# TensorE's first branch-prefetch hint stands two token pairs earlier, and the code ahead of it is aligned anew

## The reference

```python
logits = tokens @ gate_weight.T
top1 = argmax(logits); mask = one_hot(top1)
ranks = cumsum(mask, axis=0) - 1          # place of a token within its expert
mask = mask * (ranks < 320)
dispatch = gather of each expert's tokens
out = scatter( gelu(dispatch @ wi[e]) @ wo[e] * softmax weight )
```

## Time and profile before

| | |
|---|---|
| median of 3 runs | 1103.7 us (1102.2 to 1104.22) |
| the profiled execution | 1102.2 us |
| its span | 1100.5 us |
| mean granted TensorE clock | 0.978 |
| TensorE busy | 1044.6 us (95%) |
| instruction fetches on queue q8 | 31 packets, 0.51 MB |

### The profile page before, as it was taken

One profiled execution on the slowest core, in us unless ns is written; L12 is line 12 of the kernel. 1 busy time (PEld: TensorE's weight loads), 2 busy tenths in 40 slices (PEclk: granted clock), 3 DMA queues, 4 the chain that ended last, 5 costly groups with the idle time before them and its releaser, 6 DMA issues.

```text
span 1100.5 us, 20923 instructions
## 1 busy us (share of the span) xinstructions
PE 1044.6 (95%) x7912; PEld 989.0 (90%) x7912; DVE 721.5 (66%) x1089; ACT 543.9 (49%) x851; POOL 147.4 (13%) x135
## 2 busy tenths in 40 slices
PE   7699999999999999599999996999999999999995
PEld 5699999999999999378777766999999999999995
DVE  7556565776577686478685765557767677665652
ACT  5345455565556565263332224455656656554431
POOL 2201111203021110100000022002112031130101
PEclk9799999999999999899999998999999999999998
DMA  8468546565464750500011235436566565654410
GB/s 308 175 229 309 183 168 211 193 219 205 159 233 158 256 200 38 177 1 1 1 39 39 77 106 186 145 123 243 181 229 228 191 243 179 226 211 144 170 38 24
DMA packets 83280, 177.38 MB, mean 161 GB/s; under 512 B 4192, under 2 KB 4704, under 8 KB 83168
## 3 DMA queue, kind: packets, MB, share of 16 engines
q1 hardware_dynamic: 75488, 152.61, 39.1%
q0 software_dynamic: 7168, 23.07, 5.8%
q10 hardware_dynamic: 576, 1.05, 0.3%
HBM read 162.04 MB, written 18.87 MB: 164 GB/s over the span
## 4 chain that ended last, share of the span: by engine, by line
PE 92%; DVE 2%; DMA 2%; ACT 1%; issue 1%; POOL 1%; POOLq 0%; SPq 0%; ACTq 0%; DVEq 0%
PE psH L1213 13%; PE psH L1214 13%; PE psH L1215 13%; PE acc L1220 12%; PE acc L1221 12%; PE acc L1222 12%; PE acc L1213 3%; PE acc L1215 3%; PE acc L1214 3%; PE psT L1433 1%; PE psT L1269 1%; PE acc L1389 1%; PE psH L1389 1%; PE psT L1538 1%; PE psH L1440 1%
## 5 line engine op out<-in xcount | busy, mean ns | idle before, releaser
L1213 PE MATMUL psH<-dth,wih 128*128 128x240 f32 (+5 forms) x1024 | 294.6, 288 | 0.0
L1220 PE MATMUL acc<-hth,woh 128*128 128x240 f32 (+5 forms) x1024 | 293.4, 287 | 0.0
L1221 PE MATMUL acc<-htl,woh 128*128 128x240 f32 (+5 forms) x1024 | 293.2, 286 | 0.0
L1222 PE MATMUL acc<-hth,wol 128*128 128x240 f32 (+5 forms) x1024 | 293.2, 286 | 0.0
L1215 PE MATMUL psH<-dth,wil 128*128 128x240 f32 (+5 forms) x1024 | 293.2, 286 | 0.0
L1214 PE MATMUL psH<-dtl,wih 128*128 128x240 f32 (+5 forms) x1024 | 293.1, 286 | 0.0
L787 DVE TENSOR_TENSOR wol<-raw_wo,woh 128x1024 fp32r<-128x1024 f32 x128 | 155.7, 1223 | 146.6 <-ACT woh L609 146.6
L643 ACT ACTIVATE gel<-psH 128x320 f32<-128x320 f32 x256 | 111.9, 437 | 188.9 <-PE psH L1215 183.7
L609 ACT ACTIVATE woh<-raw_wo 128x1024 fp32r<-128x1024 f32 x128 | 134.3, 1056 | 132.3 <-PE acc L1222 132.2
L1213 PEld LDWEIGHTS psH<-dth,wih 128*128 128x128 f32 x1024 | 192.8, 188 | 0.3
L1220 PEld LDWEIGHTS acc<-hth,woh 128*128 128x128 f32 x1024 | 192.8, 188 | 0.0
(11 more groups left out here) (194 smaller groups left out, 1151.3 us busy)
## 6 DMA issues: line engine op xcount, KB each, us to landing
raw_wi<-in_wi SPq DMA_DIRECT2D x64, 1024.0 KB, 5.1
raw_wo<-in_wo SPq DMA_DIRECT2D x64, 1024.0 KB, 5.4
out_x<-xt SPq DMA_DIRECT2D x4, 1024.0 KB, 5.8
xt<-in_x SPq DMA_DIRECT2D x6, 512.0 KB, 8.0
xt<-x SPq DMA_DIRECT2D x3, 1024.0 KB, 10.5
raw_u<-in_wuT SPq DMA_DIRECT2D x1, 1024.0 KB, 10.8
raw_u<-in_wvT SPq DMA_DIRECT2D x1, 1024.0 KB, 12.5
xt<-in_x ACTq DMA_DIRECT2D x2, 256.0 KB, 3.4
```

Source lines behind the costliest of these rows:

```text
L1213: pe.matmul(out, lh, rh, start=first, stop=False)
L1220: pe.matmul(out, lh, rh, start=False, stop=False, skip_group_check=True)
L1221: pe.matmul(out, lh, rl, start=False, stop=False, skip_group_check=True)
L1222: return pe.matmul(out, ll, rh, start=False, stop=False, skip_group_check=True)
```

## The change

Hint 1 is marked at `p == 4` instead of `p == 6`, and the alignment constant goes from 35 to 153:

```diff
-TO_HINT = 35
+TO_HINT = 153
...
                         if p >= 2:
                             folds(p - 2)
-                        if p == PAIRED - 2:
+                        if p == 4:
                             peek()
```

## The result

The kernel after takes 1110.25 us (median of 5 runs, 1107.79 to 1110.61), the kernel before 1103.45 us (5 runs beside them, 1102.11 to 1104.22). The ratio is 1.0059, with a 95% interval of 1.0045 to 1.0075: 6.8 us more, where I had forecast 2.4 us less. The profiled execution of the kernel after took 1108.56 us, with a span of 1106.8 us and a mean granted clock of 0.975.

The account below looks back on a forecast made before the run. TensorE bounds the kernel; only its stall ahead of the first expert can shrink. Short branch 1 gives -2.4 us, alignment and thinner visit cover cost nothing: 1103.7 to 1101.3 us, range 1100.1 to 1105.6, the forecast's own 1100.1 to 1103.1.

Parts of the forecast that it names:

- The hint is served in time: Ahead of branch 1: hint at about 12.6, packet between 19.1 and 22.0, so the branch is short; chance 0.50.
- The range I took: Wait of the visit's fetch behind its hint while DMA engines are full: 6.5 to 9.4 us.
- The step that failed: At the boundary 17 instructions behind branch 1: block C, asked for at 10.3, is there in time; cost nothing.
- rival C: Behind branch 1: hint replaces block C's request, a stall of 2.7 us beside a late branch, 1106.4 us; chance 0.12.
- rival D: Ahead of L1389: remaining visits bind, 1.5 us for two visits, 0.9 us of gain left, 1102.8 us; chance 0.04.
- a cap: At L863: of the 4.13 us stall only 2.4 us can be had, the rest becomes a wait for VectorE.
- if the clock falls all the same: Table products ahead of the first expert: even if the granted clock drops to half, the gain stays 2.4 us.
- Rival A: At branch 1: hints bring nothing, the branch asks for its block itself and waits as before, 1103.7 us; chance 0.18.

Follow-up runs that it names:

- e3: Kernel before with hint 1 at p = 4 and alignment constant 205, so the hint is 7 instructions past a block boundary; 1110.54 us, ratio 1.0066.
- e12: Kernel after with the third and fourth visits of the first FFN exchanged; 1121.68 us, ratio 1.0179.
- e9: Kernel after without the fourth visit of the first FFN; 1108.42 us, ratio 1.0048.
- e6: Kernel before with branch 1 moved behind take_counts(), hint 1 and alignment kept; 1103.07 us, ratio 1.0009.
- e10: Kernel before without the fourth visit of the first FFN; 1101.21 us, ratio 0.9986.

## Why the prediction was wrong

- **The hint is served in time: right, and sooner than I put it.** The hint was expected at 12.6 and stands at 12.5; branch 1 takes 0.33 us. But its packet starts at 16.31, 3.8 us after it, not after 6.5 to 9.4 us. It is 3.8 us again in e3 (16.81 to 20.56) and in e12, and 3.7 us in e9, with a DMA share of 1.04 to 1.05 each time, as before. The range I took, 6.5 to 9.4 us, was too late; two more kernels with the hint where it was before, e6 and e10, have 5.6.
- **The step that failed** is the sentence "block C must be in the store when the boundary behind branch 1 is passed ... It is asked for at 10.3 and has 12 us. This costs nothing." It wasn't fetched at all until the return from the visit. I had the sign of it in the earlier trace rows, where block L wasn't fetched while hint 1 was pending, and weighed it as rival C with 0.12, since the hint is 2.2 us younger than the boundary. The runs show that 2.2 us isn't enough for the block's own request to get ahead, and that it is ahead when the hint stands 80 instructions in or more.
- **Rival C happened, and was priced too low.** Its 2.7 us were to stand beside a branch as long as before. From the return's end (22.84) it took 1.8 us to the first packet (24.67), 2.5 us until both packets, side by side, were done (27.20), and 1.7 us to the eighth product (28.92): 6.1 us, of which the seven products cover 0.6, so 5.46 us of stop. Branch 1 is short as well, so `earlier()` starts 3.56 us sooner (23.09 for 26.65), and 1.9 us are left at L1308.
- **What lies behind L1308.** The table products take 6.27 us for 5.80 us, 0.5 us more; the clock, at half from 28.6 to 32 before, stays there until 34.9. The stretch 32 to 35.4 after, columns as in the earlier trace rows:

```profile
32.00:35.40 3.40, 3.40 (x20) 3.40 (x20) 2.83 (x3) 0.00 (x0) 0.67 (x1) 0.58 0.03 5
```

  The last normalized rows are ready 2.6 us later than before, and then the visits bind, as rival D had it: the sequencer's L1479, at 40.6 in the earlier trace rows, is behind them now, at 44.9, since branches 3 and 4 took 4.4 and 3.4 us. That is the last 0.5 us of 3.12.

```profile
L1479 PEldq FUSED_REGOPS  x1: 53/53/53, 44.9 to 44.9; - x1
```

- **Nothing in the prediction held the 4.1 us at the third expert.** I let the effect on the store end with the first expert. 2.56 us of it is the miss, the rest the clock at half for 3.4 us after the stop.
- **The gain had a cap that I had seen, and it was too high.** I put 2.4 us on a short branch 1. The kernel with the visit behind the counts has no stop at all, and its ratio is 1.0009. The 2.4 us are there at L863, but I let everything behind it move along by the same amount, also "if the clock falls all the same". In fact the table products wait 0.7 us for VectorE and take 0.5 us more at the low clock, and 1.1 us arrive at L1389. In 13 of the 14 kernels a packet starts between 22.4 and 25.5 us, hint or not, which is about where the DMA share falls from 1.0; that it is what bounds this stage was only argued, not tried.
- **Rival A's half truth.** Where it stood, hint 1 made branch 1 no shorter, though leaving it out costs 0.2% (1.0022 [1.0011, 1.0033]). But hints aren't dead: in the kernel with the visit behind the counts the hint turns 3.7 us into 0.33.

The Trainium skill's page "Runtime: NRT & Kernel Launch", section "Instruction fetch mechanics", has prefetch as purely sequential. The trace after disagrees: the packet at 16.31 is followed by a visit of 328 ns to a block that isn't next, and the next one is missing.

What stays open: which block the store gives up, and why the order visit before C costs the block of width 272 much later. It was tried through the number and the order of visits alone. It is the larger half: 4.1 us of the loss.

## What to carry to other kernels

In these runs a prefetch hint was not an extra fetch: while the DMA engines were full, it took the place of the fetch of the code's own next block. So check that the block behind the branch is there as well. Shift a hint and an alignment together only with the boundaries drawn in: distance from the last boundary to the hint, and from the branch to the next one. After such an edit read every branch over 1 us in the whole trace, not only those near it, because the price may come 130 us later.

## What the runs showed of the hardware

- A branch whose block is in the store takes 0.2 to 0.4 us, one that has to wait for its block 2.2 to 4.4 us in these kernels, and 6.3 us once, in the kernel with the exchanged visits.
- Two instruction packets side by side take 1.55 and 2.18 us in the kernel after, one alone 0.9 to 1.5, in the first stretch mostly 1.09. A branch that waited for a packet ends about 1.4 us after it (24.26 to 25.72 in the kernel before).
- While the DMA share is about 1.0, the fetch of a hinted block started 3.7 to 3.8 us after its hint in the four kernels where it is the first packet of block B, and 5.6, 5.6 and 6.5 us after it in three (e6, e10, before) where block C's packet had started 3.3 to 3.4 us ahead of the hint.
- After a stop of 2.56 us in the middle of dense products the granted clock fell to half from 161.2 to 164.6, though TensorE had taken up its work at 160.93.
- Moving one hint instruction by 86 places, with the alignment to it, changed the time by 0.6%; exchanging two visits changed it by 1.2 points more.
